# Two graph-attention layers: edge sums by TensorE over 128-edge tiles, or by VectorE running sums along 128 chunks

## What is computed

```python
feat = (h @ W).reshape(n, H, F)                  # H = 4 heads, F = 64
el, er = sum(feat * al), sum(feat * ar)          # one number per node and head
e  = leaky_relu(el[src] + er[dst], 0.2)
m  = segment_max(e, dst);  ex = exp(e - m[dst])
a  = ex / segment_sum(ex, dst)[dst]
out = segment_sum(feat[src] * a, dst) + b;  out = elu(out)
```

## Time and profile before

| what | us |
|---|---|
| median of three runs (8819.84 to 8861.85) | 8845.29 |
| the profiled execution, time | 8804.24 |
| the profiled execution, span | 8802.4 |

### The profile page before, as it was taken

How to read it: one execution, slowest core, us unless ns; L and a number is a source line. 1 busy time by engine, 2 the same in 40 slices (tenths; PEclk the granted TensorE clock), 3 DMA queues, 4 the chain that set the end, 5 groups by cost and what they waited for, 6 DMA issues and landing times. The chain is left out here.

```text
span 8802.4 us, 84021 instructions
## 1 busy us (share of the span) xinstructions
PE 4858.6 (55%) x17856; PEld 3338.1 (38%) x17856; DVE 4457.3 (51%) x6896; ACT 3274.2 (37%) x8056; POOL 5368.2 (61%) x5389
## 2 busy tenths in 40 slices
PE   3577776766667669344444444448444444444441
PEld 3344444443444356233333333335233333333330
DVE  5578887877778765233333333343133333333336
ACT  2466666666666543122222222222122222222222
POOL 3556666655556544666666666647566666666656
PEclk8788888888888889667766766667566676676665
DMA  7555555554555477566666666653466666666666
GB/s 212 153 159 165 165 165 155 163 153 146 152 154 169 145 191 222 170 185 186 190 181 187 189 187 182 186 150 95 134 191 181 183 190 188 190 179 189 188 185 185
DMA packets 1205795, 1526.63 MB, mean 173 GB/s; under 512 B 255529, under 2 KB 1027186, under 8 KB 1205196
## 3 DMA queue, kind: packets, MB, share of 16 engines
q1 hardware_dynamic: 952300, 846.59, 30.1%
q0 software_dynamic: 253408, 679.03, 29.0%
HBM read 789.66 MB, written 735.67 MB: 173 GB/s over the span
## 5 line engine op out<-in xcount | busy, mean ns | idle before, releaser
L1774 POOL DMA_INDIRECT gb_g<-table,ix_g x3136 | 2997.2, 956 | 1546.8 <-issue 906.2
L1803 PE MATMUL po<-gb_g,sel_g 128*128 128x256 f32 x6272 | 2038.5, 494 | 1924.8 <-issue 1065.1
L1803 PEld LDWEIGHTS po<-gb_g,sel_g 128*128 128x128 f32 x6272 | 1542.1, 253 | 2384.1 <-issue 1790.1
L630 POOL DMA_INDIRECT gb<-table,ix x1568 | 1641.6, 1047 | 1068.8 <-DMA ix<-in_src_cols 539.7
L1841 ACT ACTIVATE ost_g<-po 128x512 f32<-128x512 f32 x1568 | 920.8, 598 | 2988.6 <-DMA x<-in_x 1570.4
L661 PE MATMUL po<-msg,sel 128*128 128x256 f32 x3144 | 966.4, 461 | 701.0 <-ACT ost L728 416.3
L1893 DVE TENSOR_TENSOR sel_g<-lastpos,pI 128x512 f32<-128x512 f32 x784 | 533.6, 681 | 1251.9 <-issue 777.0
L661 PEld LDWEIGHTS po<-msg,sel 128*128 128x128 f32 x3144 | 681.3, 228 | 954.7 <-issue 708.2
L1897 DVE TENSOR_TENSOR gb_g<-gb_g,pW 128x1024 f32<-128x1024 f32 x784 | 952.1, 1214 | 0.0
L1857 DVE TENSOR_TENSOR_SCAN fs<-start_f,pW 128x128 f32<-128x128 f32 (+1 forms) x98 | 41.2, 421 | 1258.0 <-PE pW L1782 784.8
L721 ACT ACTIVATE pt<-pt,sh 128x128 f32<-128x128 f32 x1568 | 440.7, 357 | 382.1 <-remote 196.1
(11 more groups left out here) (275 smaller groups left out, 5311.3 us busy)
## 6 DMA issues: line engine op xcount, KB each, us to landing
sums<-ost_g SPq DMA_DIRECT2D x784, 528.0 KB
sums<-ost SPq DMA_DIRECT2D x393, 512.0 KB
gb_g<-table,ix_g POOLq DMA_INDIRECT x3136
gb<-table,ix POOLq DMA_INDIRECT x1568
table<-f SPq DMA_DIRECT2D x48, 520.0 KB
x<-in_x SPq DMA_DIRECT2D x50, 256.0 KB
at<-in_rbf SPq DMA_DIRECT2D x100, 128.0 KB
hT_d<-hT SPq DMA_DIRECT2D x49, 256.0 KB
```

Source lines behind the costliest of these rows:

```text
L630: eng.indirect_dma_start(out=gb[:, g, j, :, :].rearrange("p a c -> p (a c)"), out_offset=None, in_=q.table0[:, :], in_offset=bass.Indirect ...
L1774: eng.indirect_dma_start(out=gb[:, p, j, :], out_offset=None, in_=q.table1[:, :], in_offset=bass.IndirectOffsetOnAxis(ap=ix[:, p, j:j + 1] ...
L1803: ins = eng.matmul(po[2 * (k % 2) + x][:, j, :], sel[:, k % 4, 2 * x + j, :], gb[:, p, tl, 0:D], start=True, stop=True)
```

## The change

1. **gat_edges**: partition p owns the 1,568 neighbouring edges p*1568 to p*1568+1567 (a chunk). A superblock is 32 columns of all chunks. The gathers stay 32 per superblock with 128 rows each. `gb` has three buffers and rows of 264. TensorE isn't used. VectorE makes weights, then runs 32 steps in which row t becomes `row(t-1) * same(t) + row(t)`, in place in `gb`, and SP stores from `gb`, four columns at a time (128 x 4 rows, now 4 neighbouring rows in memory per partition). All inputs of VectorE's instructions lie in SBUF.
2. **chunk_stitch** replaces stitch for the GAT layers: 128 chunk ends, one gather and one scatter.
3. **Masks**: structure ends without them; layer0_nodes makes the new ones (three of 128 x 6,468, bfloat16) in 16 steps beside pairs 9 to 24. It loads x into five buffers, and each load now stands ahead of the store of `hT_d` on SP's list.
4. **Bias**: the one-row matmuls are gone; VectorE adds the bias when it copies the features from PSUM, in ScalarE's place.
5. Smaller initial fills in layer0_edges; node_edges turns one more small tile.

The core of the diff (chunk_stitch in part):

```diff
@@ gat_edges, gpsimd
+                def body(s, i, p):
...
+                    eng.wait_ge(s_ix[p].sem, s_ix[p].at(i))
+                    eng.wait_ge(s_st[p].sem, s_st[p].at(i, back=1))
+                    eng.wait_ge(s_sum.sem, s_sum.at(s, 1, back=2))
+                    for j in range(SBT):
+                        eng.indirect_dma_start(out=gb[:, p, j, 0:FR], out_offset=None, in_=q.table1[:, :],
+                                               in_offset=bass.IndirectOffsetOnAxis(ap=ix[:, p, j:j + 1], axis=0)).then_inc(s_g[p].sem, 16)
@@ gat_edges, scalar
+                    eng.activation(ww[:, :, :], ee[:, :, :], ACT.Exp).then_inc(s_w.sem, 1)
+                    eng.wait_ge(s_den.sem, s_den.at(s))
+                    for k, y in enumerate((dn, mm_)):
+                        ins = eng.activation(gb[:, p, :, D + k * H:D + (k + 1) * H], y[:, :, 1:].rearrange("p h t -> p t h"), ACT.Copy)
@@ gat_edges, vector (one superblock)
+                    k_same = own(eng.tensor_copy(same[:, :], q.samep[:, here]))
+                    k_in = own(eng.tensor_copy(ee[:, :, 0:1], mm_[:, :, SBT:W]))
+                    eng.wait_ge(s_g[p].sem, s_g[p].at(i))
+                    k_el = own(eng.tensor_tensor(ee[:, :, 1:], rows[:, :, D:FR].rearrange("p t h -> p h t"), held[:, :, here], ALU.add))
+                    k_el = own(eng.scalar_tensor_tensor(ee[:, :, 1:], ee[:, :, 1:], 0.2, ee[:, :, 1:], ALU.mult, ALU.max))
+                    k_fs = own(eng.tensor_tensor_scan(flat(fs), add_m, flat(ee), -BIG, ALU.add, ALU.max))
+                    k_mm = own(eng.tensor_tensor_scan(flat(mm_)[:, ::-1], back_m, flat(fs)[:, ::-1], -BIG, ALU.add, ALU.max))
+                    eng.tensor_tensor(ee[:, :, :], ee[:, :, :], mm_[:, :, :], ALU.subtract).then_inc(s_d.sem, 1)
+                    eng.wait_ge(s_w.sem, s_w.at(s))
+                    k_acc = own(eng.tensor_tensor(acc[:, :].rearrange("p (h c) -> p h c", c=C),
+                                                  gb[:, (p - 1) % B, SBT - 1, 0:D].rearrange("p (h c) -> p h c", c=C),
+                                                  ww[:, :, 0:1].to_broadcast([P, H, C]), ALU.mult))
+                    def weighted(k):
+                        f = rows[:, 4 * k:4 * k + 4, 0:D].rearrange("p t (h c) -> p t h c", c=C)
+                        w = ww[:, :, 1 + 4 * k:5 + 4 * k].rearrange("p h t -> p t h")
+                        return own(eng.tensor_tensor(f, f, bc(w, 3, [P, 4, H, C]), ALU.mult))
+                    k_w = weighted(0)
+                    k_dn = own(eng.tensor_tensor(ww[:, :, 0:1], ww[:, :, 0:1], dn[:, :, SBT:W], ALU.mult))
+                    eng.tensor_tensor_scan(flat(dn), mul_m, flat(ww), 0.0, ALU.mult, ALU.add).then_inc(s_den.sem, 1)
+                    for k in range(NQ):
+                        after(k_w)
+                        for j in range(4):
+                            t = 4 * k + j
+                            behind = acc[:, :] if t == 0 else rows[:, t - 1, 0:D]
...
+                            ins = eng.scalar_tensor_tensor(rows[:, t, 0:D], behind, same[:, t:t + 1], rows[:, t, 0:D], ALU.mult, ALU.add)
...
+                            if j == 0 and k + 1 < NQ:
+                                k_next = weighted(k + 1)
@@ gat_edges, sync
+                        eng.wait_ge(s_sum.sem, s_sum.at(s, k))
+                        eng.dma_start(out_v[s * NQ + (k - 1), :, :, :], gb[:, p, 4 * k - 4:4 * k, :]).then_inc(s_st[p].sem, 16)
@@ chunk_stitch
+                eng.dma_start(tl[:, :], q.sums1.rearrange("(p e) c -> p e c", p=P)[:, CH - 1, :]).then_inc(s_tl, 16)
...
+                eng.indirect_dma_start(out=hd[:, :], out_offset=None, in_=q.sums1_x, in_offset=col(q.chunk_head, 0)).then_inc(s_hd, 16)
+                eng.wait_ge(s_fin, 1)
+                eng.indirect_dma_start(out=q.sums1_x, out_offset=col(q.chunk_fix, 0), in_=hd[:, :], in_offset=None,
+                                       bounds_check=EP - 1, oob_is_err=False).then_inc(s_fix, 16)
...
+                eng.tensor_tensor_scan(cm[:, 1:], add_w[:, :], pm[:H, 0:P], -BIG, ALU.add, ALU.max).then_inc(s_cm, 1)
...
+                for j in range(2):
+                    eng.tensor_tensor_scan(cb[:, j, 1:], pf[:, j * P:(j + 1) * P], tT[:, j, :], 0.0, ALU.mult, ALU.add).then_inc(s_cb, 1)
@@ layer0_nodes, sync and vector
+                        if i + XB < NPAIR:
+                            eng.wait_ge(s_z, i + 1)
+                            eng.dma_start(x[i % XB][:, :, :], xin[i + XB, :, :, :]).then_inc(s_x[i % XB], 16)
                         eng.wait_ge(s_h, i + 1)
...
+                        eng.tensor_tensor(q.samep[:, :], c0[:, :], c1[:, :], ALU.is_equal).then_inc(s_seg, 1)
+                    elif x <= H:
+                        eng.tensor_copy(muls[:, :, x - 1, 1:], along)
+                    elif x <= 2 * H:
+                        eng.tensor_scalar(adds[:, :, x - H - 1, 1:], along, BIG, -BIG, ALU.mult, ALU.add)
+                    elif x <= 3 * H:
+                        eng.tensor_scalar(backs[:, :, x - 2 * H - 1, 1:], along[:, :, ::-1], BIG, -BIG, ALU.mult, ALU.add)
...
+                    if 9 <= i < 9 + 3 * H + 4:
+                        segments(i - 9)
@@ layer0_norm_and_gat_nodes, tensor and vector (gat_output the same)
-                            eng.matmul(pF[:, i, 0:GR], hT[g % 2][:, j, i * P:(i + 1) * P], we[:, j, :], start=j == 0, stop=False)
-                        ins = eng.matmul(pF[:, i, 0:GR], q.unit[:, 0:P], bias[:, :], start=False, stop=True)
+                            ins = eng.matmul(pF[:, i, 0:GR], hT[g % 2][:, j, i * P:(i + 1) * P], we[:, j, :], start=j == 0, stop=j == 1)
...
+                    eng.tensor_tensor(f[g % 2][:, 0:m, :], pF[:, 0:m, 0:GR], bc(bias[:, :], 1, [P, m, GR]), ALU.add).then_inc(s_f, 1)
```

More of the change, by code:

```diff
@@ L260, in _ @@
                         dst[:, g0 * TP:g1 * TP].rearrange("p (g t) -> p g t", t=TP), ps[x % 2][:, 0:g1 - g0, 0:TP])))
[L261 to L274, removed]
+                eng.wait_ge(dv.sem, made["lay"][-1])
             @block.sync
@@ L317, in layer0_nodes @@
     a, sb, pb = q.a, q.sb, q.pb
-    B = 3
+    line = a["dst_line"]
+    B, XB, W = 3, 5, SBT + 1
     with ExitStack() as c:
         wup = sb(c, "wup", [P, 2, P])
-        x = [sb(c, f"x{b}", [P, 2, D]) for b in range(B)]
+        x = [sb(c, f"x{b}", [P, 2, D]) for b in range(XB)]
         z = [sb(c, f"z{b}", [P, 2, D]) for b in range(2)]
@@ L327, in layer0_nodes @@
         up = [sb(c, f"up{b}", [P, 2, D]) for b in range(B)]
+        lead = sb(c, "lead", [P, CH])
+        first, base, cut = (sb(c, n, [P, 1]) for n in ("first", "base", "cut"))
+        c0, c1 = (sb(c, n, [P, CH], I32) for n in ("c0", "c1"))
         pT = [pb(c, f"pT{b}", [P, 2, 2 * P]) for b in range(2)]
@@ L1381, in _, with normed @@
                     eng.wait_ge(s_we, k + 1)
-                for g in range(NQUAD):
+                def normed(g):
                     b, m = g % 2, size(g) // 2
@@ L1604, in _, with results @@
                         eng.wait_ge(s_we, k + 1)
+                def results(g):
+                    m = size(g)
+                    eng.wait_ge(s_pF, g + 1)
+                    if g >= F:
+                        eng.wait_ge(s_tab[g % F], 32 * times(g - F, F))
+                        eng.wait_ge(s_sc[g % F], moved(g - F, F))
+                    eng.tensor_tensor(f[g % F][:, 0:m, :], pF[:, 0:m, 0:GR], bc(bias[:, :], 1, [P, m, GR]), ALU.add).then_inc(s_f, 1)
                 scaled(0)
-                for g in range(NQUAD):
+                for g in range(NQUAD + 2):
                     if g + 1 < NQUAD:
                         scaled(g + 1)
-                    elu(g)
+                    if g < NQUAD:
+                        elu(g)
+                    if n == 1 and g > 1:
+                        results(g - 2)
             @block.scalar
@@ new lines, in _ @@
+                eng.sem_inc(dv.sem, dv.base)
+                eng.sem_inc(s_sum.sem, s_sum.base)
+                eng.memset(gb[:, B - 1, SBT - 1, 0:D], 0.0)
+                eng.memset(dn[:, :, :], 0.0)
+                eng.memset(mm_[:, :, :], -BIG)
+                eng.wait_ge(s_ini, 16)
+                eng.wait_ge(s_ch, 16)
+                for h in range(H):
+                    ins = eng.tensor_tensor_scan(held[:, h, :], q.samep[:, :], ch.rearrange("p (e h) -> p e h", h=H)[:, :, h], ini[:, h:h + 1], ALU.mult, ALU.add)
+                    ins.then_inc(s_held, 1)
@@ L1905 @@
+                eng.wait_ge(s_held, H)
+                with eng.Fori(0, SB // B) as i:
+                    for p in range(B):
+                        body(i * B + p, i, p)
+                body(SB - 1, SB // B, 0)
 def kernel(**inputs):
```

666 lines of the change are left out of this document (272 added, 394 removed).

## The result

The changed kernel takes 8,511.49 us (median of 8,490.31 to 8,519.2) against 8,832.57: ratio 0.9631, 95% interval 0.9594 to 0.9668. Forecast was 8,515, range 8,260 to 8,740. The profiled execution has a span of 8,488.6 us, before 8,802.4: 313.8 less.

What follows compares the result with a forecast made beforehand. POOL's gathers and its waits for landings and TensorE, not bandwidth, were taken to bound the GAT edges. Terms -117, -107, -46, -10, -40, -10 sum to -330: 8,474 us profiled, 8,515 as median; range 8,260 to 8,740.

Steps and rivals of the forecast that it cites:

- Period and port: GAT edges: POOL alone sets a superblock's period, 45.0 us; gathers held by VectorE instructions with two SBUF inputs, 0.156 us each.
- the meeting: GAT edges: gathers start at random against VectorE's instructions, so the delay is the sum of h²/2 over P.
- the price of a lock: GAT edges, bound from above: VectorE's steps line up with gathers, half of all wait 0.37 us, period 45.9 us.
- The exclusion rival: GAT edges: VectorE waits for gathers as well, 52.3 us a superblock, about 9,230 us; slower, by this or similar, 0.07.
- The undelayed rival: GAT edges: gathers go almost undelayed, period 43.1 us (8,329) or 40.0 (8,025); chance 0.13.
- Edges: GAT edges, both layers: 2,251 us a layer against 2,311 and 2,308, together -117 us.
- Stitch: Stitches of both GAT layers: about 20 us each in place of 73.8, together -107 us.
- Structure: Structure stage: six long mask passes and their loads go, -46 us.
- Masks: First node stage: 16 mask steps cost up to +29 us, earlier x loads give back up to -40; taken at -10.
- Bias: GAT nodes' stage: a group of four tiles takes 7.4 us in place of 9.1, -40 us (0 to -55).
- Output: GAT output: removed matmuls lie mostly beside POOL's indirect transfers, -10 us (0 to -40).
- Layer 0's fills: Layer 0's edges: the changed initial fills give under 5 us, taken at nothing.

Runs made afterwards that it cites:

- run 1: Changed kernel with VectorE's weights and weighted products in PSUM (also written e1): 8,842.04 us, ratio 1.0002.
- 2: Changed kernel with only the weights moved to PSUM, products still written to SBUF: 8,781.46 us, ratio 0.9935.
- run 3: Changed kernel with 16 weighted products of two rows in a superblock in place of eight of four: 8,634.42 us, ratio 0.9767.
- run 9: e8 with two empty sequencer instructions ahead of three steps in four: 7,938.05 us, the kernel before 7,579.15, ratio 1.0473.
- Run 4: Changed kernel with three buffers for x in place of five in the first node stage: 8,490.08 us, ratio 0.9592.
- Run 7: Changed kernel with four buffers in place of three for x and the layer-0 output in the GAT nodes' stage: 8,500.41 us, ratio 0.9635.
- 5: Changed kernel with two row buffers in place of three, in three variants: e7 8,694.12 us, e8 8,507.53, weights alone in PSUM 8,657.66.
- e8: Changed kernel with two buffers for the rows in place of three, all operands in SBUF: 8,507.53 us, ratio 0.9607.
- run 8: e7 with a small POOL memset ahead of each gather, 8,658.77 us, or each second one, 8,698.83; the kernel before took 8,966.73.
- e7: Changed kernel with weights and products in PSUM and two buffers for the rows in place of three: 8,694.12 us, ratio 0.9829.

## Why the prediction was right, and how far

**Period and port: right in the hold, lucky in the meeting.** The waits went, the gathers were held by what was left of one VectorE instruction less about 0.12, VectorE was not held, and the period was 45.5 for 45.0. Runs 1 and 2 show the hold by itself: same work and transfers, one input moved to PSUM, mean 0.952, and 0.950 beside the products alone. The sum let gathers meet instructions at random, and they don't. In a superblock the same eight gathers start inside products and wait 0.50 each, the same eight inside steps and wait 0.16: 5.3 us, where chance gave 5.0. That the two agree so closely is luck; the price of a lock, 45.9, stood in the prediction as the bound from above. Where the instructions are other in size or start at other times, the delay is 0.130 for 0.097 (run 3) and 0.193 a gather (run 9, nearly the same instructions). The exclusion rival (9,230) is out, by VectorE's durations above. Of the rule of the Trainium skill ("SBUF — State Buffer", section "Who interferes with whom") these rows agree with the two SBUF inputs as the condition and with a gather that comes second; a VectorE instruction that comes second was not blocked in any row here (670 products that start inside a gather last 1.222 us at most). The undelayed rival is out for this kernel too.

**Edges: right, 13 us a layer too low**: 49 x 0.45 = 22 by the period, less 9 at the start and the tail.

**Stitch: right, sized 7 us each too dear**: 13.5 for 20.

**Structure: right.** **Masks: right sign, -26.8 for -10.** The steps do cost (pairs with one follow each other at 4.25 us, later ones at 3.3), but outside them the stage is faster than the 4.1 of before. Run 4 shows that this is not the five buffers; that it is the load ahead of the store is what remains of the edit, and is argued, not shown.

**Bias: mis-sized, -23.9 for -40.** The matmuls went, but the transfers are the next bound, as far as the share tells: I took 6.1 to 7.1 us of transfer for a group, and at a share near 0.9 they take 8 to 9. Run 7 shows that earlier loads don't help. Part of the miss is this one execution: the same code takes 229 to 233 us in ten other traces, which would be -32 to -36. **Output: right**, -14.9 for -10. **Layer 0's fills**: +10.8 lies within what the same code varies by.

**The sum.** These errors cancel in part: 52 us too little gained (edges, bias, layer 0), 36 more than forecast (masks, stitch, output and small ones). The profiled executions differ by 314 for 330; that the median came out 4 us from the forecast is luck, since the profile of after lies 21 us under its median, and the 41 of before had been added.

**What the prediction didn't see** is why the old waits were there. It took POOL's waits for landings as the old loop's own, from its four-slot ring of stores. SP's register additions in the old loop, min/median/max:

```profile
L1734 SPq ALU_OP  x672: 2/33/1398, 3618.8 to 8542.7; - x168
```

Their maximum is 1.398 us, where a median is 0.033, and 182 of the 672 additions last over 0.6: SP, which issues those stores, was stretched in the kernel before too. Measured together with run 9, whose trace has no stretches, the kernel before is 1,260 us shorter. The record lists chip 8 for these measurements and for those of runs 1 to 4, where the kernel before took 8,840, so the chip alone doesn't decide it. Layer 0's edges are 591 of that shorter in the variant (2,135 to its stitch against 2,726), which is code that both share; most of the other 670 must then lie in the old GAT edges, about 300 a layer, which would be 41 us a superblock (an estimate; no trace of the kernel before was taken there). The changed loop gains nothing from the absence: its gathers are held by VectorE at 45.5 us a superblock in the changed kernel and at 46.25 in run 9. That the stretches made the old waits is argued from this and not shown. So the gain that was forecast and measured stands beside stretched instructions; without them a near variant of the change is 4.7% slower, and the changed kernel itself, at 45.4 in place of 46.25, would be at about 7,938 - 98 x 0.85 = 7,855, 3.6% slower (an estimate, not run).

**Left open**: what stretches the instructions. Shown is that it reaches SP, VectorE and POOL; that in runs 1, 2 and 5 (without e8) it begins some 8 to 55 us into 64 gathers which follow each other at 1.25 us and nearly always ends within 10 us of the last of them; and that run 9 was free of it. Of VectorE's register instructions beside the GAT edges 15 of 5,248 last over 0.6 us in the changed kernel, 2,244 of 5,248 in run 1, 1,387 of 6,016 in run 3, 536 and 1,627 of 5,376 in run 8. Neither the gathers' length nor their spacing puts these in order.

No variant beat the changed kernel by more than the intervals: with two buffers, 8,507.53, it is the same at a third less memory for the rows.

## What to carry to other kernels

Before work is moved to VectorE beside a stream of gathers, count its instructions with two SBUF inputs and charge the stream half of each one's square over the period, as a first estimate: here gathers and instructions ran in step, and the same kind of sum was off by a third in run 3. A PSUM input takes that charge away. But look then at the sequencers' own lines: an engine that needs many short waiting instructions per gather can lose more than the port gave. And a gain that consists of waits removed is worth only as long as what caused the waits is there, which should be read from the issuing queue's own rows before it is counted.

## What the runs showed of the hardware that was not expected

Sequencer instructions of SP and VectorE of 0.04 us take 0.70 us each, on ticks common to both (in e1 both engines have one that starts at 4260.3, at 4274.3 and at 4281.3), while gathers start 1.25 us apart. In e7 SP's store instruction (line 1727), first from 4072, soon after the gathers begin again at 4067.7, then from 4096:

```profile
L1727 SPq DMA_DIRECT2D sums<-gb_g x2: 302/400/499, 4072.3 to 4075.3; - x2
...
L1727 SPq DMA_DIRECT2D sums<-gb_g x2: 709/710/710, 4097.7 to 4104.7; - x2
```

In the changed kernel, whose gathers VectorE holds a little by accident, VectorE hardly shows it; freeing them by 0.17 us each cost 8,842 - 8,511 = 331 us. And the same kernel took 8,840 us, or 7,579 beside the one trace without stretches.
